# First expert layer: GpSimd issues a token tile's pair of indirect DMAs only after the pair two tiles earlier has landed

## What is computed

```python
probs = softmax(flat @ gate_W)                    # 8 experts
topk_w, topk_idx = top_k(probs, 2)                # two experts per token
topk_w = topk_w / topk_w.sum(axis=-1, keepdims=True)
combine = (one_hot(topk_idx, 8) * topk_w[..., None]).sum(axis=1)
out = 0.5 * gelu(flat @ shared_W + shared_b)
for e in range(8):
    h = gelu(flat @ W1[e] + b1[e])
    out = out + combine[:, e:e + 1] * (h @ W2[e] + b2[e])
out = layernorm(out) * gamma + beta               # then x = layernorm(x + out)
```

## Time and profile before

| | before |
|---|---|
| time, median of three runs | 1735.92 us (1734.03 to 1738.34) |
| span of the profiled execution | 1877.1 us |
| TensorE busy in the span | 1375.8 us (73%) |
| VectorE | 1255.0 us (67%) |
| ScalarE | 874.9 us (47%) |
| GpSimd | 931.8 us (50%) |
| indirect DMAs of the layer, scatter L1034 / gather L1047 | 64 / 64 |

### The profile page before, as it was taken

One profiled execution on the slowest core, in us unless ns is written; L12 is line 12 of the kernel. 1 busy time (PEld: TensorE's weight loads), 2 busy tenths in 40 slices (PEclk: granted clock), 3 DMA queues, 4 the chain that ended last, 5 costly groups with the idle time before them and its releaser, 6 DMA issues. The chain is left out here.

```text
span 1877.1 us, 25647 instructions
## 1 busy us (share of the span) xinstructions
PE 1375.8 (73%) x7305; PEld 741.0 (39%) x7305; DVE 1255.0 (67%) x2478; ACT 874.9 (47%) x1616; POOL 931.8 (50%) x858
## 2 busy tenths in 40 slices
PE   6848888888888839497614589999899899603628
PEld 2323333333333739396512234443343343202524
DVE  6999999999975302041385698889889886251215
ACT  5856566666656215163314046655555556402320
POOL 1579898989850450604235112223453454765640
PEclk8969999999899759598768699999999999856768
DMA  1046000000000426365414111110110103032215
GB/s 50 0 172 230 1 0 1 0 0 0 0 0 13 119 72 177 90 185 153 117 36 135 58 55 52 40 43 28 56 68 31 45 32 93 11 51 70 78 60 194
DMA packets 124235, 122.67 MB, mean 65 GB/s; under 512 B 29522, under 2 KB 102463, under 8 KB 121720
## 3 DMA queue, kind: packets, MB, share of 16 engines
q1 hardware_dynamic: 102292, 97.47, 17.4%
q0 software_dynamic: 10240, 15.79, 2.9%
q10 hardware_dynamic: 11588, 8.01, 1.3%
HBM read 76.68 MB, written 50.52 MB: 68 GB/s over the span
## 5 line engine op out<-in xcount | busy, mean ns | idle before, releaser
L1992 DVE TENSOR_REDUCE t_negm<-t_ps 128x1 f32<-128x512 f32 (+4 forms) x624 | 369.3, 641 | 57.1 <-PE t_ps L2261 35.7
L1967 ACT ACTIVATE t_PT<-t_ps_s 128x1024 f32<-128x1024 f32 (+3 forms) x384 | 294.5, 811 | 239.5 <-PE t_ps_s L2280 231.0
L464 POOL TENSOR_TENSOR s_HC<-s_H,X 128x1024 f32<-128x1024 f32 x128 | 307.3, 2419 | 39.6 <-DVE s_H L585 29.7
L2261 PE MATMUL t_ps<-heads 128*128 128x512 bf16 (+3 forms) x768 | 233.3, 340 | 66.5 <-DVE t_identb L1985 36.7
L629 PE MATMUL ps_y<-s_HC,ident 128*128 128x512 f32 x512 | 265.9, 644 | 21.2 <-POOL s_HC L464 19.8
L1899 POOL TENSOR_SCALAR_AFFINE_SELECT t_PT<-t_PT 128x512 f32<-128x512 f32 x128 | 84.3, 660 | 310.3 <-ACT t_PT L1967 309.9
L2280 PE MATMUL t_ps_s<-heads 128*128 128x512 bf16 (+3 forms) x768 | 180.7, 328 | 9.9 <-issue 4.5
L1082 ACT ACTIVATE f_HT<-f_ps_h,f_b 128x128 f32<-128x128 f32 x340 | 96.6, 371 | 180.8 <-remote 115.7
L2295 PE MATMUL t_ps_c<-t_PT,t_VG 128*32 128x512 f32 (+3 forms) x1536 | 164.6, 502 | 1.5 <-POOL t_PT L1899 1.2
L2261 PEld LDWEIGHTS t_ps<-heads 128*128 128x128 bf16 x768 | 73.3, 99 | 231.6 <-DVE t_negm L1992 149.1
L1047 POOL DMA_INDIRECT f_YG<-expert_rows_out,f_idx_s x64 | 64.5, 1008 | 191.1 <-DMA expert_rows_out<-f_YB 172.5
(11 more groups left out here) (327 smaller groups left out, 2450.1 us busy)
## 6 DMA issues: line engine op xcount, KB each, us to landing
f_w<-in_W_dram SPq DMA_DIRECT2D x93, 256.0 KB
y_Y<-token_expert_rows SPq DMA_DIRECT2D x8, 1024.0 KB, 12.3
token_expert_rows<-X SPq DMA_DIRECT2D x42, 192.0 KB, 2.5
heads<-qk_parts SPq DMA_DIRECT2D x42, 192.0 KB
heads<-qk_parts SPq DMA_DIRECT2D x14, 576.0 KB
qk_parts<-p_parts SPq DMA_DIRECT2D x48, 128.0 KB, 2.9
expert_rows<-X SPq DMA_DIRECT2D x27, 192.0 KB, 2.4
f_XS<-expert_rows SPq DMA_DIRECT2D x19, 256.0 KB, 3.4
```

The costliest lines, as they stand in the source:

```text
L464: nc.gpsimd.tensor_tensor(HC[:, g % RING], H[:, g % RING], row_wide(C_sb[:, g % RING, :], 2), ALU.mult).then_inc(s_hc, 2)
L1967: nc.scalar.activation(PT[:, n % RP, 2 * p:2 * p + 2, 0:wd], src, ACT.Exp, scale=DK ** -0.5).then_inc(s_exp, 1)
L1992: nc.vector.tensor_reduce(out, ps_1[use % BANKS1][:, 0:h * width].rearrange("p (h k) -> p h k", h=h), AX.X, ALU.max, negate=True).then_inc ...
L2261: mm = nc.tensor.matmul(out[:, u * width:(u + 1) * width], Q[g][:, j + u, qt * P:(qt + 1) * P], K[g][:, j + u, c * CH:c * CH + width], sta ...
```

## The change

`FLIGHT = 2` is new. Each scatter semaphore of a group becomes two, for even and odd tiles. POOL waits before a tile's pair, from the third tile of a group on, until the pair of two tiles before has landed; the same is done in `gather` with the semaphores that are there. Whoever waited for a group's scatter waits for both semaphores now.

```diff
+FLIGHT = 2
...
 def rows_in(q):
                 if j == 0:
-                    sp.wait_ge(s_sc[g], 16 * 2 * (GROUPS[g][1] - GROUPS[g][0]))
+                    for x in range(FLIGHT):
+                        sp.wait_ge(s_sc[g][x], 32 * (GROUPS[g][1] - GROUPS[g][0]) // FLIGHT)
...
 def scatter(g):
                 for t in range(lo, hi):
+                    if t - lo >= FLIGHT:
+                        pool.wait_ge(s_sc[g][t % FLIGHT], 32 * ((t - lo) // FLIGHT))
                     for r in range(2):
                         pool.indirect_dma_start(out=xs[g], out_offset=...,
                                                 in_=X1t[:, t, :], in_offset=None, bounds_check=GBLK[g] * P - 1,
-                                                oob_is_err=False).then_inc(s_sc[g], 16)
+                                                oob_is_err=False).then_inc(s_sc[g][t % FLIGHT], 16)
...
 def gather(g):
                 for t in range(lo, hi):
                     if t >= RG:
                         pool.wait_ge(s_add, 2 * PER * ((t - RG) // PER + 1))
+                    if t - lo >= FLIGHT:
+                        pool.wait_ge(s_g[(t - FLIGHT) % RG], 32 * turns(t - FLIGHT, RG))
...
 def combine(i):
-                dve.wait_ge(s_sc[g], 16 * 2 * (GROUPS[g][1] - GROUPS[g][0]))
+                for x in range(FLIGHT):
+                    dve.wait_ge(s_sc[g][x], 32 * (GROUPS[g][1] - GROUPS[g][0]) // FLIGHT)
```

More of the change, by code:

```diff
@@ L2735, in build @@
         keep = dict(ones=sb("mean_ones", [P, P]), eps=sb("eps", [P, 1]), one=sb("one", [P, 1]), ident=sb("ident", [P, P]))
-        keep["s_dispatched"] = [ctx.enter_context(nc.semaphore(f"dispatched{g}")) for g in range(NGR)]
+        keep["s_dispatched"] = [[ctx.enter_context(nc.semaphore(f"dispatched{g}_{x}")) for x in range(FLIGHT)] for g in range(NGR)]
         keep["s_gathered"] = [ctx.enter_context(nc.semaphore(f"gathered{r}")) for r in range(RG)]
```

## The result

| | before | after |
|---|---|---|
| time, median of five runs each | 1736.38 us (1734.03 to 1738.34) | 1745.38 us (1742.78 to 1749.5) |
| span of the profiled execution | 1877.1 us | 1744.7 us |

The ratio is 1.0050, with a 95% interval of 1.0036 to 1.0064: the change costs 9 us. The forecast was 1739 us, and its range of 1733 to 1749 us holds the time; the likeliest outcome named there, a difference too small to tell, did not come.

A forecast was written before the change was run, and what follows sets the result against it. Timed runs were taken as bound at scatter(1) and gather(1), without the profile's slow stretches. 31 path waits at 0.2 us gave 6.2 us, halved to 3 us: 1735.92 + 3 = 1739 us, range 1733 to 1749 us.

The forecast's parts named there:

- the slow stretches: First expert layer: four stretches, 123 us, with few PE matmuls beside POOL's DMAs; 108 us excess, taken as absent from timed runs.
- The rule of the Trainium skill: The block taking instruction records pushes back on engines when a FIFO fills; the change could alter only the profile.
- if the stretches vanish and the time stays, the cap acts on the recording alone: Sign in the changed kernel's profile: span falls, time stays; then the profiled-versus-timed reconciliation also holds.
- counted by half: Half of scatter(0)'s 6 waits put on the path, with 14 each in scatter(1) and gather(1): 31 waits.
- the rule for a free wait: POOL's wait is free if the second DMA lands within 2.7 us (gather) or 2.6 us (scatter); anything beyond is lost.
- the price of a wait: POOL's waits on landings: 0.2 us each, over 31 path waits 6.2 us.
- six samples: Second DMAs of pairs, three scatters and three gathers, landings counted in packets; three late, 1.1 to 1.2 us together.
- taking half of it: The 6.2 us over path waits cut to 3 us, since a late pair gives the next wait slack.
- the transposes of group 1's first quad: PE waits there for all of scatter(1) and a load; each microsecond more of scatter(1) is one of the end.
- The second rival: Waits bind more often in scatter(1) and gather(1), pairs late by 0.3 to 0.5 us: 12 us, 1748 us; chance 0.22.
- Landings as in attention: Scatter(1), gather(1), gather(2): landings near 5.0 us, 1.1 us more a pair, 44 us, 1780 us; chance 0.04.
- a gain from a cured stretch: Slow stretches are real and the cap ends them: gain 27 us (1709 us) to 108 us (1628 us); chance 0.12.

The follow-up runs named there:

- the cap on scatters alone: The changed kernel with POOL's waits on landings kept in the scatters only (26 of 52): 1740.16 us against 1736.27 us, ratio 1.0024.
- that on gathers alone: The changed kernel with POOL's waits on landings kept in the gathers only (26 of 52): 1740.95 us against 1736.27 us, ratio 1.0037.
- cap one: The changed kernel with FLIGHT = 1, each pair waiting for the one before it: 1861.56 us, ratio 1.0706.
- Caps of three and four: The changed kernel with FLIGHT = 3 or 4, waiting on the pair three or four tiles earlier: 1737.32 us (ratio 1.0001) and 1736.30 us (1.0004).
- before, profiled again: The unchanged kernel, profiled a second time: 1735.11 us against 1735.49 us, ratio 0.9990, span 1735.9 us.
- the kernel with only the semaphores split: The changed kernel without POOL's 52 waits on landings, split semaphores and SP and DVE waits kept: 1736.25 us against 1736.27 us, ratio 0.9996.
- lighter loads: From the seventh block, 128 of 512 w1 columns loaded: changed kernel 1735.07 us (0.9989 to before), kernel before 1730.41 us (0.9968).

## Why the prediction was right or wrong

**Right: the slow stretches belong to the profiled execution.** The step from 1877.1 to 1735.92 us was the largest in the working, 141 us, and the timed runs of both kernels bear it out. Wrong was the reason given and what followed from it, that the stretches come whenever every instruction leaves a record, and would be there again at a span near 1877 us. They were in none of ten further profiles. The rule of the Trainium skill that was weighed there (NOTIFIC — the notification-queue block, section 7.1) would have the timed runs left alone; they became 9 us slower, by another cause, and no run here shows that mechanism. The histogram was misread as well: the 6, 1, 4, 5, 8, 9, 9, 9 that the prediction gives for the layer are slices 20 to 27, of which the layer has only the first two. The prediction's reading "if the stretches vanish and the time stays, the cap acts on the recording alone" would have been wrong too: they vanish without the cap as well.

**Right: where it costs.** scatter(1) and gather(1) carry the cost, and scatter(2), gather(0) and gather(2) none. In gather(0) and scatter(2) POOL lost 1.9 and 3.0 us, and these were covered. With the cap on scatters alone the second stage is as short as before, and with that on gathers alone the first; only cap one uses up the cover of scatter(2) and gather(0). gather(2)'s waits are met: its 19.7 us did not change. Nothing came from the split semaphores. scatter(0) was counted by half; POOL lost 0.8 us in it (scatter(1) starts 21.7 us after scatter(0) with the cap, 21.3 us without), and what of this reached the end was not measured by itself.

**Right: the rule for a free wait.** Only what a landing takes beyond the bound counts. Counted to the last packet, as the prediction does, the bound is 3.84 - 0.76 - 0.35 = 2.7 us, against its 2.6 to 2.7; counted to the signal it is 3.1 to 3.2 us. Caps of three and four, whose bounds lie above all but the rarest landings, cost nothing.

**Wrong: the price of a wait.** The term was 0.2 us a wait from six samples, three of them late by 0.3 to 0.4 us. The share that is late was right (13 of 28 bind). Their size was not: 0.08 to 2.13 us, 0.85 us in the mean, so 11.1 us over the 28 waits, 0.40 us each and twice the estimate. Why the samples misled is argued, not shown. It is not that they lay in the slow stretches: the DMA engines' share was 0.43, 0.66 and 0.75 in the three windows of the earlier trace rows, and in before, profiled again, it is 0.44, 0.81 and 0.77 at the start of scatter(0), at that of gather(0) and over gather(1). But three of the six are of scatter(0), the lightest place, where POOL lost 0.8 / 6 = 0.13 us a wait, and none is of scatter(1) or lies beyond the third pair of a burst. All but the first DMAs of scatter(1) and gather(1) stood in slow stretches with shares of 0.16 and 0.27, where it is 0.65 and 0.77 in before, profiled again, so that the trace at hand couldn't show their landings. The one landing of 5.0 us in the trace of before was set aside as attention's, though landings of 5.2 and 5.0 us belong to this layer.

**Wrong: taking half of it.** "A delay is not paid twice" describes what happens on POOL: the wait at 671.82 lost 2.13 us, and the next one nothing. But this is in the measured 0.40 us already. What the halving should have stood for is the part that the path absorbs. POOL lost 0.8 us in scatter(0) and 5.4 us in scatter(1), of which 3.1 us reached the start of gather(1), give or take the 1.4 us by which single traces differ; it lost 5.7 us in gather(1), and 5.7 us reached gather(2). The prediction had PE wait in a timed run at the transposes of group 1's first quad, so that each microsecond of scatter(1) is one of the end. Before, profiled again, shows no pause there. In the changed kernel the first to wait is not those transposes but `up` of block 20, on weights that stand behind the late load:

```profile
689.04 1.91 PE L1418 MATMUL f_ps_h<-f_XT,f_w 128*128 128x128 f32 x8 [2.19 <-issue]
```

The load is 5.5 us late and the pause 2.2 us, so PE had some 3 us of slack here, and the pause is most of the stage's 3.1 us. With the cap on scatters alone the same pause is 0.7 us, as in the kernel with only the semaphores split, though the stage is 3.8 us longer, so the way of these microseconds through PE is not settled.

**The sum, corrected.** 28 waits x 0.40 us = 11.1 us on POOL, less 2.3 us of scatter(1)'s that did not reach the stage's end: 8.8 us, against 9.0 measured. The 2.3 us is what is left between POOL's loss and the stage, 5.4 - 3.1, so this sum is the account of a trace and not a test of it. The test is that the timed runs, which it does not use, agree. The second rival (31 waits of 0.4 us, 12 us, 1748 us) was closer than the forecast. Its condition, more than 0.17 us a path wait paid in full, was met at 9.0 / 31 = 0.29 us. The range held the time because it took in most of this rival. The forecast's own 3 us are a third of the 9 us: a wait was priced at half, and the sum halved again. Landings as in attention, at 1.1 us a pair, did not come, and neither did a gain from a cured stretch.

**A page's figure.** The Trainium skill (DMA: Bandwidth & Descriptors, Anatomy of one DMA — SWDGE path) led to an estimate of 2.15 us for such a DMA. The traces agree with it as a floor: the shortest gather took 2.5 us to land, with lighter loads 2.4 us, and the shortest scatter 2.2 us. The fit has no term for other traffic, and landings beyond the bound, up to 5.2 us in the changed kernel, are the whole cost.

## What to carry to other kernels

A cap on what is under way costs nothing as long as the time between a transfer's start and the wait for it (the number of pairs under way times their pace) is above the slowest landing, not the mean one. Compute it before capping, and expect up to a microsecond of the end for each one that is lost on a path stage: here it was 5.7 of 5.7 us in one and about half in the other. Take samples of a landing where the traffic is that of the timed run, and take enough of them to see the tail.

When a profiled span is longer than the timed median by more than its scatter, profile the unchanged kernel again before anything in the odd stretches is read, since a stretch that is gone in the next profile may be gone without the change too.

## What the runs showed of the hardware

One profiled execution ran 141 us longer than the timed runs, with PE and the DMA engines nearly still in four stretches in which GpSimd issued indirect DMAs. The same kernel profiled again took 1735.9 us, and POOL's scatters take 978 ns in the median in both. What set off the slow stretches is unknown.

Indirect DMAs of 128 rows of 512 bytes land 2.2 to 5.9 us after they start, where landings are marked in the traces of this layer, and once 6.1 us. In before, profiled again, they land later the more traffic is beside them: medians of 2.5, 3.4 and 4.2 us at DMA shares of 0.17, 0.77 and 0.90. The mean share of a stage hides the worst of it. It is 0.63 over scatter(1) and 0.70 over gather(1) in the changed kernel, but 0.87 and 0.73 in the 6 us in which the landings of 5.2 and 5.0 us fell.

From the signal of such a landing to the start of the DMA that GpSimd held back for it 0.76 us pass, the same in the scatters that wait with caps of one and of two pairs.
